# A fused decoder block on one core: where the experts' first-layer weights are fetched from

## What is computed

```python
x = layernorm(x + attention(x))                     # causal, 16 heads of 64, one shared key/value head
x = layernorm(x + cross_attention(x, ctx_768))      # 16 heads of 64, context of 96 values a token
# the expert layer: 8 experts, each token goes to its best 2
scores = x @ Wr.T + br
idx    = top_k(scores + biases_N, 2)
val    = softmax(scores)[idx];  val = val / val.sum()
h      = x @ Wl1[e] + bl1[e]                        # Wl1[e]: 128 x 512
y_e    = (silu(h[:, :256]) * h[:, 256:]) @ Wl2[e] + bl2[e]
x = layernorm(x + sum over the 2 experts of val * y_e)
```

## Time and profile before

| | us |
|---|---|
| median of 3 runs | 843.4 |
| lowest, highest | 843.33, 844.18 |
| span of the profiled execution | 876.8 |

### The profile page before, as it was taken

One profiled execution on the slowest core, in us unless ns is written; L12 is line 12 of the kernel. 1 busy time (PEld: TensorE's weight loads), 2 busy tenths in 40 slices (PEclk: granted clock), 3 DMA queues, 4 the chain that ended last, 5 costly groups with the idle time before them and its releaser, 6 DMA issues.

```text
span 876.8 us, 26473 instructions
## 1 busy us (share of the span) xinstructions
PE 797.6 (91%) x9276; PEld 659.0 (75%) x9308; DVE 621.1 (71%) x1834; ACT 593.9 (68%) x1444; POOL 453.7 (52%) x441
## 2 busy tenths in 40 slices
PE   3799999999999988999999999999998979879996
PEld 2577787878777767887888888878786867768862
DVE  4877887878788757898787878878788534334425
ACT  2677888888788756677777767767675555446535
POOL 5477676776767732222535353535343455555543
PEclk9899999999999999999999999999999898999998
DMA  8499999000000000000000000000000445557636
GB/s 259 86 154 161 155 157 126 1 0 0 0 0 0 2 1 7 7 7 7 24 13 22 15 22 16 22 15 19 19 19 28 147 144 173 180 168 218 205 126 232
DMA packets 69392, 64.79 MB, mean 74 GB/s; under 512 B 5702, under 2 KB 54985, under 8 KB 69168
## 3 DMA queue, kind: packets, MB, share of 16 engines
q1 hardware_dynamic: 62592, 51.42, 29.0%
q0 software_dynamic: 4624, 9.61, 3.2%
q10 hardware_dynamic: 2080, 2.49, 0.9%
HBM read 35.37 MB, written 28.58 MB: 73 GB/s over the span
## 4 chain that ended last, share of the span: by engine, by line
PE 52%; issue 18%; POOL 12%; DVE 8%; ACT 5%; DMA 2%; another core or an unknown queue 2%; POOLq 0%; SPq 0%; ACTq 0%; DVEq 0%
PE bank L1813 8%; PE bank L1709 7%; PE bank L1509 5%; POOL rq L533 5%; PE bank L1511 5%; PE bank L1510 5%; PE bank L1823 3%; POOL PR L538 3%; PE bank L1684 3%; PE bank L1697 3%; PE bank L1585 2%; PE bank L1803 2%; PE bank L1593 2%; ACT VBD L393 2%
## 5 line engine op out<-in xcount | busy, mean ns | idle before, releaser
L393 ACT COPY VBD<-bank 64x512 f32<-64x512 f32 x192 | 111.3, 580 | 28.3 <-PE bank L1511 25.5
L570 POOL TENSOR_TENSOR PR<-PR,rL 128x1024 f32<-128x1024 f32 x32 | 60.9, 1904 | 115.0 <-DVE rL L1119 114.8
L533 POOL TENSOR_TENSOR rq<-ssq,mhalf 128x17 f32<-128x17 f32 x32 | 99.3, 3102 | 15.6 <-DVE ssq L968 15.1
L632 POOL DMA_INDIRECT zbuf<-PT,KT x71 | 69.7, 982 | 65.7 <-ACT PT L894 32.4
L538 POOL TENSOR_TENSOR PR<-PR,rL 128x1024 f32<-128x1024 f32 x32 | 61.0, 1906 | 82.4 <-DVE rL L999 82.4
L1440 DVE SCALAR_TENSOR_TENSOR stage<-bank,b_now,early 128x128 f32<-128x128 f32 x142 | 43.3, 347 | 77.1 <-ACT early L886 42.5
L1813 PE MATMUL bank<-xT,w_now 128*128 128x128 f32 x568 | 82.0, 291 | 1.1
L622 POOL DMA_INDIRECT xbuf<-xg,slot x64 | 65.2, 1018 | 34.1 <-DVE xg L1314 21.6
L886 ACT ACTIVATE early<-bank,b_now 128x128 f32<-128x128 f32 x142 | 44.7, 368 | 52.5 <-PE bank L1813 37.9
L1813 PEld LDWEIGHTS bank<-xT,w_now 128*128 128x128 f32 x568 | 77.1, 209 | 3.3 <-issue 3.2
L802 ACT ACTIVATE PT<-bank 128x512 f32<-128x512 f32 x64 | 38.3, 600 | 43.5 <-PE bank L1697 41.7
(11 more groups left out here) (252 smaller groups left out, 2312.6 us busy)
## 6 DMA issues: line engine op xcount, KB each, us to landing
w_now<-in_wl SPq DMA_DIRECT2D x71, 256.0 KB
xbuf<-blank SPq DMA_DIRECT2D x1, 17160.0 KB, 119.6
KT<-xbuf SPq DMA_DIRECT2D x71, 65.0 KB
VBD<-zbuf SPq DMA_DIRECT2D x4, 512.0 KB, 5.0
out<-X SPq DMA_DIRECT2D x8, 256.0 KB, 2.3
cT<-in_ctxT ACTq DMA_DIRECT2D x16, 96.0 KB, 1.9
zbuf<-PT,KT POOLq DMA_INDIRECT x71
wl_sb<-in_wl POOLq DMA_DIRECT2D x1, 1024.0 KB, 9.2
```

The costliest lines, as they stand in the source:

```text
L393: u = copy(VBD[h * SEQ:(h + 1) * SEQ, p, s, lo:lo + blocks, :], bank[CHUNK_BANK[c]][s * SEQ:(s + 1) * SEQ, :].rearrange("k (a d) -> k a d" ...
L533: nc.gpsimd.tensor_tensor(rq[:, :], ssq[:, :], mhalf[:, 0:HEADS + 1], ALU.pow).then_inc(a["pow"], 1)
L632: nc.gpsimd.indirect_dma_start(out=zbuf, out_offset=at, in_=yb[:, t % YB, :], in_offset=None, bounds_check=K2 * TOK - 1, oob_is_err=False) ...
```

## The change

The first-layer weights of all eight experts (128 partitions x 4096 numbers, 2 MB) are loaded once into `arena` (`wl1_sb`), after self-attention's last tile has released it. SP no longer loads a tile's block. GpSimd copies the block from `wl1_sb` into the ring `w_now` instead, in its slot i for tile i+2, ahead of the put of tile i-3. GpSimd now reads the expert numbers into registers too, and SP no longer does. PE waits on one counting semaphore instead of four. The ring keeps its four buffers.

```diff
+        wl1_sb = arena[:, 0:NE * 2 * HID].rearrange("p (n h) -> p n h", n=NE)
...
+            sp.wait_ge(a["yS"], T)
+            sp.dma_start(wl1_sb[:, :, :], wl1).then_inc(w_l1, 16)
...
                     numbers(mybir.EngineType.SP, row_tab, xbuf.shape[0] - P, t, first_row)
-                    expert_numbers(mybir.EngineType.SP, t, expert)
...
-            def load_weights(t, q):
-                if later(t, JB):
-                    sp.wait_ge(hs["L1"], t - JB + 1)
-                sp.dma_start(w_now[:, q, :], wl1[:, bass.ds(expert[t], 1), :].rearrange("d n h -> d (n h)"))\
-                  .then_inc(hs[f"w{q}"], 16)
-
             def slot_tile(i, q):
                 of_tile(load_rows, i, q, -4)
-                of_tile(load_weights, i, q, -3)
...
+            def weights_now(t, q):
+                if t == 0:
+                    pool.wait_ge(w_l1, 16)
+                    pool.wait_ge(f["tableA"], TABLE_A)
+                if t == J_A:
+                    pool.wait_ge(f["tableB"], TABLE_B)
+                if t % EB == 0:
+                    expert_numbers(mybir.EngineType.Pool, t, known)
+                if later(t, JB):
+                    pool.wait_ge(hs["L1"], t - JB + 1)
+                pool_copy(w_now[:, q, :], wl1_sb[:, bass.ds(known[t], 1), :].rearrange("p n h -> p (n h)"))\
+                    .then_inc(hs["w"], 1)
...
             def slot_tile(i, q):
+                of_tile(weights_now, i, q, -2)
                 of_tile(put, i, q, 3)
...
-                pe.wait_ge(hs[f"w{q}"], 16 * (t // JB + 1))
+                pe.wait_ge(hs["w"], t + 1)
```

More of the change, by code:

```diff
@@ L232, in decoder @@
         staged, split, consts = sem("staged"), sem("split"), sem("consts")
-        zeroed, w_ids = sem("zeroed"), sem("w_ids")
+        zeroed, w_ids, w_l1 = sem("zeroed"), sem("w_ids"), sem("w_l1")
         slices = []
@@ L263, in decoder @@
         hs = {n: sem("h_" + n) for n in (
-            "x0", "x1", "x2", "x3", "w0", "w1", "w2", "w3", "T1", "xT", "L1", "b1_now", "silu", "gT",
+            "x0", "x1", "x2", "x3", "w", "T1", "xT", "L1", "b1_now", "silu", "gT",
             "L2", "y", "yb", "put0", "put1", "put2", "put3", "put4", "put5", "put6", "put7", "b1")}
@@ L428, in _ @@
             sp.dma_start(b1_sb[:, :, :], bl1).then_inc(hs["b1"], 16)
-            expert, first_row = {}, {}
+            sp.wait_ge(a["yS"], T)
+            sp.dma_start(wl1_sb[:, :, :], wl1).then_inc(w_l1, 16)
+            first_row = {}
             def load_rows(t, q):
@@ L633, in put @@
                                              bounds_check=K2 * TOK - 1, oob_is_err=False).then_inc(hs[f"put{t % YB}"], 16)
+            def weights_now(t, q):
[10 more added lines that the diff above has]
+                    .then_inc(hs["w"], 1)
+            known = {}
             def slot_tile(i, q):
+                of_tile(weights_now, i, q, -2)
                 of_tile(put, i, q, 3)
```

## The result

| | us | ratio to before |
|---|---|---|
| before, 4 runs beside it | 843.6 (843.33 to 844.18) | |
| after, 4 runs | 888.55 (886.83 to 890.19) | 1.0515, 95% interval 1.0489 to 1.0541 |
| forecast | 903.0, range 868 to 918 | |

(The ratio is the one on record for this comparison; the quotient of the two medians, 1.0533, lies within its interval.) The profiled execution of after took 889.55 us at a span of 887.8: its time is the span and 1.75 us more.

A forecast was written before the change was run, and what follows sets the result against it. PE bounds the kernel at 1.76 us a tile; GpSimd would become the bound at 2.36. From 698.10, 155.8 + 6.4 + 15.4 + 6.0 = 183.6 gives span 909.4, less 5.9 is 903.5 us; range 868 to 918.

The forecast's parts named there:

- tile 40: Expert loop: its rows, 4.8 us after the last send starts, come before tile 39's copy ends at 6.8; adds nothing.
- the signs named beforehand: Copy 1.0 to 1.1 us, GpSimd back to back at 2.3 to 2.4, PE waiting 0.6 a tile, span 900 to 920.
- The copy: GpSimd's 128x512 block copy, interpolated from 128 and 1024 columns: 1.05 us, between 0.41 and 1.90.
- The pace: GpSimd per tile: 1.05 copy + 0.17 gap + 1.02 put + 0.03 + 0.09 wait and address = 2.36 us.
- The 8 register loads: GpSimd's loads of expert numbers, 0.60 each with 0.15 of gap: 6.0 us.
- The start: GpSimd runs without a pause from 698.10 us, where the send before the first put ends, with tile 5's copy.
- From the profile to the median: Profiled span 33.4 us above the median: 27.5 only in the profiled execution, 5.9 staying in both kernels; 909.4 - 5.9 = 903.5.
- the holes: Expert tiles 5 to 70: late semaphore signals, 30 us beyond PE's pace; 27.5 put down to the profiled execution.
- What goes: 71 weight loads and 9 register loads leave SP's queue: worth nothing while GpSimd is the bound.
- The cold clock: TensorE at 1.2 GHz, 2.74 us a tile: 25 us more over the whole stage, 928; within a rival of 11%.
- Rival 1: Expert stage: the late signals are in timed runs too, GpSimd's path only 32.6 us longer: 876; 27% with a cheaper variant.
- Rival 3: GpSimd keeps up, needing copy and gaps in 0.48 us or less: 816 at best or no change; 4%.

The follow-up runs named there:

- experiment 2: Changed kernel with a second GpSimd copy of each block into a spare ring nobody reads: 959.88 us, ratio 1.1344.
- experiment 3: Changed kernel with the block copy on VectorE in place of GpSimd: 844.05 us, ratio 0.9969; in a second set 844.06 us, 0.9971.
- experiment 8: Changed kernel with GpSimd's copy as a plain one-operand copy in place of a product with ones: 856.42 us, ratio 1.0121.
- experiment 9: Changed kernel with VectorE copying the blocks of tiles 0 to 39 and GpSimd, by plain copy, those of 40 to 70: 844.6 us, ratio 0.9968.
- experiment 1: The kernel before, unchanged, profiled again (the second trace of before): 847.23 us, span 845.4.
- experiment 7: Kernel before with the 2 MB load added and not used, the 71 loads of 256 KB kept: 846.07 us, ratio 1.0006.
- experiment 10: Kernel with the copy on VectorE, plus a second VectorE copy into a spare ring nobody reads: 845.16 us, ratio 0.9984.

## Why the prediction was right, and what was off by how much

**The mechanism held.** The transfer was hidden, GpSimd became the bound, PE followed the copies, the ring never filled, and tile 40 added nothing (its copy follows in 2.26 us like the others). Experiments 2, 3, 8 and 9 show it from four sides: double the copy and nearly the whole of it is added, take it off GpSimd and the whole loss goes, make it shorter and the time follows until PE's 1.76 us, place it where GpSimd has room and it is free. Of the signs named beforehand, the copy's duration, the queue without idle time and the 0.6 us a tile ahead of the first layer's weight loads (42.5 us for 71) came; the pace (2.3 to 2.4) and the span (900 to 920) did not, for the sizes below.

**The copy** was 1.05 us as worked out from the earlier trace rows, where the bounds were 0.41 and 1.90. The Trainium skill's "GPSIMD Engine Reference", section "Performance versus the Vector engine", would have had an estimated 1.12; the trace decides for 1.05. The same section explains its rate by one read port used in turn for two inputs. Experiment 8 agrees: with one input the copy is 0.63 us. I had not asked whether the product with ones was the cheapest form of a copy, and that was worth 32 of the 45 us (33 of 43 by the ratios).

**The pace** was mis-sized: 2.36 forecast, 2.25 measured. The 0.09 us for wait and register address was none (0.02 from a put to the next copy holds both), and the put 1.01. On 66 copies that is 7.3 us. These and the register loads are the terms of the sum that were mis-sized.

**The 8 register loads** were counted at 6.0 us and cost nothing. They show at 572 ns each in the trace of after, on GpSimd's queue, but no tile of the saturated stretch is longer for them: they ran beside the copies and puts in front of them. With the rest as forecast (the trace has the 66 copies, 5 puts over and 12 sends of the sum), 66 x 2.25 + 5 x 1.27 + 12 x 1.28 = 170.2 us, from the copy of tile 5 at 689.69 to the end of the last put at 858.93 + 0.97 = 859.9.

**The start** of that stretch was forecast at 698.1 and came at 689.7. Of these 8.4 us, 4.4 belonged to that one long execution: its expert stage began at 684.9, that of the second trace at 680.5. In the traces of the kernels behind the change it began between 676.4 and 681.0, in that of experiment 7, which keeps the 71 transfers, at 676.9. So the two groups cover the same stretch, and nothing shows that the change moves the start. That such starts differ by 4 us from one execution to the next I had no trace to know; what sets them stays open.

**From the profile to the median** I took 27.5 us of the holes as the profiled execution's own, and left 5.9 us as a surplus of every profile. The first half was right: the expert stage of the second trace is 26.9 us shorter. The second was wrong in sign. The time of a run is its span and 1.75 to 1.8 us more (after, and experiment 1), so the whole 33.4 us, and 1.8 more, was that one long execution. The Trainium skill's "Runtime: NRT & Kernel Launch", section "The launch sequence", has the profile's total above the timed execution by about 6.2 us. The span used here is another figure, from the first instruction to the last, and it lies below the time; the page's gap was no term for it. The reason that I gave, traffic of the records, fell too: the second trace of before carries the same records and has no such holes.

The terms together: forecast 903.5, less 13.4 for the path (7.3, 6.0 and rounding), less 8.4 for the start, plus 7.7 for the surplus (5.9 and 1.75) is 889.4; the profiled run had 889.55. The surplus had the opposite sign to the other two errors, 7.7 against 21.8, which is luck: without it the point would have been off by 22 and not by 14.5.

**What goes** was called worth nothing while GpSimd is the bound. Where it is not, the 71 transfers were in fact worth a little: with the copy on VectorE or ScalarE, or on both engines in turn, the kernel is 0.3% faster than before, in four comparisons (two of them against the same runs of before) whose intervals all end below 1 (with VectorE's second copy, the fifth, it ends at 1.0008). In the second trace of before, PE waits 1.3 us for a block, once, ahead of tile 39. That block's load stands in SP's queue behind the rows of tile 40, which wait for the last sends and the second table: the rows' load is issued at 753.14 us and the block's at 753.66, and PE, free from 755.40 on, starts at 756.66. Experiment 7, which keeps the transfers, has that wait at the same tile, 1.6 us:

```profile
L1818 PE MATMUL bank<-xT,w_now 128*128 128x128 f32 x568 | 75.7, 276 | 1.8 <-DMA w_now<-in_wl 1.6
```

With the copy on VectorE, on ScalarE or on two engines in turn it is 0.1. From the first layer's start to the last put's end these two traces have 137.3 and 137.9 us, the other four 135.7 (twice), 136.5 and 136.8. So about half of the 2.5 us or more is this wait; the rest I can't place within the scatter between executions. The load alone has an interval that holds 1, so it is not what brings the gain.

**The rivals.** The cold clock fell: 1.00 in all windows of the stage from 680 us on, with PE idle for up to 28% of one. It did show up in experiment 2 (0.74 at 760 to 780 us, where PE was busy for 14.21 us of 20); the time was within theory all the same. Rival 1 had a number closer in size (876 is 12.6 below the result, the forecast 14.5 above) but its cause is refuted by the second trace. Rival 3's threshold, a copy of 0.48 us, was stated with the gaps and 1.28 for the put; behind a copy the put's cost is 1.01 + 0.17, and experiment 8 puts the threshold at about 0.6 us outside the stretch with sends.

## What to carry to other kernels

Before work moves to an idle engine, sum that engine's own instructions per tile at their place in the loop, with the gaps between them, and compare with the pace of the bound. Its share over the whole span (52% for GpSimd here) did not show it; its busy time in the windows of that stage did. If the sum is over, ask first whether the operation has a cheaper form and whether another engine has the room: one word, or another engine, decided here between 5.2% slower, 1.2% slower and 0.3% faster. And before an unexplained excess of one profile over the timed runs is made a term of a sum, take a second profile.

## What the hardware showed that I had not expected

**VectorE is held up by GpSimd.** The bias copy of 128x4 numbers takes 0.16 to 0.17 us alone (0.19 on average in the second trace of before) and 0.97 on average in the changed kernel, 1.53 in most of its late tiles, and that is where VectorE's 59 us come from. The chain of waits in after even runs over it over its late tiles: a held instruction looks like work there. In the timeline of after, one that starts 0.59 us into a put (796.83 - 796.24) lasts to the end of the block copy that follows (796.83 + 1.53 = 798.36, against 797.26 + 1.06 = 798.32, in the timeline above). One that starts 0.42 us into a put is not held:

```profile
747.17 1.01 POOL L628 DMA_INDIRECT zbuf<-PT,KT  x1 [0.17 <-issue]
747.59 0.17 DVE L1443 COPY b_now<-b_sb 128x4 f32 x1 [0.21 <-DVE stage L1452]
```

Where exactly a put begins to hold it stays open: another bias copy of the same trace, at 753.35, also 0.42 us into a put, is held to the end of the block copy behind it (1.70 us). Where ScalarE copies the block and none follows on GpSimd, it lasts only to the put's end, here 788.85 in both rows:

```profile
787.87 0.98 POOL L628 DMA_INDIRECT zbuf<-PT,KT  x1 [0.78 <-ACT PT L890]
788.47 0.38 DVE L1443 COPY b_now<-b_sb 128x4 f32 x1 [0.21 <-DVE stage L1452]
```

In that trace the bias copies that start up to 0.51 us into a put or more than 0.8 us into it take 0.17, those from 0.53 to 0.75 last to its end. The plain block copy of experiment 8 holds too, when a bias copy starts inside it; its late bias copies are short because they start 0.90 us into a put (788.80, above), ahead of the block copy. From its timeline:

```profile
702.78 0.62 POOL L641 COPY w_now<-arena 128x512 f32 x1
702.82 0.62 DVE L1443 COPY b_now<-b_sb 128x4 f32 x1
```

So in part of a put, and in a block copy of either form, GpSimd holds something that VectorE needs, in full and not in shares. The Trainium skill's "SBUF — State Buffer", section "SBUF: two separate sides", calls it an exclusive lock on a port pair that the two engines share; these rows agree with it for the block copy, and show such a hold in a part of an indirect DMA's issue too. That it was not the bound follows from two readings: between 740 and 760 us of after VectorE was busy for 11.04 us only at the same 2.25 us between copies, and in experiment 8 the late tiles' bias copies take 0.17 and the time still follows GpSimd's sum.

**The other way round it cost little.** The same section warns that a plain fp32 copy on VectorE keeps GpSimd from writing its descriptors. In experiment 3 the puts have a median of 979 ns against 977 in the second trace of before, and single ones take up to 1.23 us; the mean goes from 981 to 999. With two copies on VectorE (experiment 10) the mean is 1032 and the longest 1.61 us. So the puts do get longer beside these copies, but GpSimd had room for it.
